# Shared expert blocks of a mixture-of-experts layer: VectorE's table chain cut into four steps inside one block, and two row buffers for TensorE

## The reference

```python
def _L0_ffn_ref(x, Ws1, bs1, Ws2, bs2, We1, be1, We2, be2, Wr, br):
    ys = _geglu(xf @ Ws1 + bs1) @ Ws2 + bs2          # shared expert: all 4096 tokens, hidden 512
    logits = (xf @ Wr + br) / TAU
    top_val, top_idx = jax.lax.top_k(logits, 2)      # two of 12 experts a token
    ...
    h = jnp.einsum('nd,edh->enh', xf, We1) + be1[:, None, :]     # experts: hidden 768
    act = _geglu(h)
    yE = jnp.einsum('enh,ehd->end', act, We2) + be2[:, None, :]
    yr = jnp.einsum('end,ne->nd', yE, w)
    return (ys + yr).reshape(B, T, Dm)
x = x + _L0_xattn_ref(_layernorm(x, axis=-1), ctx_1024, ctx_1024, mask_BxSxS2_bk1, ...)
x = x + _L0_ffn_ref(_layernorm(x, axis=-1), ...)
```

## Time and profile before

| | us |
|---|---|
| median of three runs | 1064.05 |
| the profiled execution, time | 1065.91 |
| its span in the trace | 1064.3 |
| TensorE busy | 948.2 (89%) |
| attention part ends, shared blocks begin on TensorE | 465.9 |
| first matmul of an expert | 587.1 |

### The profile page before, as it was taken

How to read it: one execution, slowest core, us unless ns; L and a number is a source line. 1 busy time by engine, 2 the same in 40 slices (tenths; PEclk the granted TensorE clock), 3 DMA queues, 4 the chain that set the end, 5 groups by cost and what they waited for, 6 DMA issues and landing times.

```text
span 1064.3 us, 26714 instructions
## 1 busy us (share of the span) xinstructions
PE 948.2 (89%) x7515; PEld 696.4 (65%) x7515; DVE 715.9 (67%) x1842; ACT 569.6 (54%) x1276; POOL 372.4 (35%) x537
## 2 busy tenths in 40 slices
PE   5578899999998888978899789999899999999996
PEld 4223444444453346767788678888688888888885
DVE  4776778888787654647686566776546577667753
ACT  3125555655555573323444556766546566667653
POOL 5210212254544362157000334444223444434342
PEclk9779999999999998989899989999999999999998
DMA  4552424273562131247644552545225445535232
GB/s 149 137 101 71 104 69 111 64 188 94 121 161 63 63 140 60 71 157 240 218 150 132 162 131 45 138 131 141 41 33 130 114 78 141 130 48 145 43 52 41
DMA packets 107926, 117.30 MB, mean 110 GB/s; under 512 B 20397, under 2 KB 99961, under 8 KB 107649
## 3 DMA queue, kind: packets, MB, share of 16 engines
q1 hardware_dynamic: 87168, 67.97, 24.0%
q0 software_dynamic: 20064, 47.20, 17.8%
q10 hardware_dynamic: 560, 0.53, 0.1%
HBM read 73.91 MB, written 38.87 MB: 106 GB/s over the span
## 4 chain that ended last, share of the span: by engine, by line
PE 39%; issue 5%; DMA 5%; DVE 4%; ACT 1%; DVEq 1%; SPq 1%; ACTq 1%; POOL 0%; POOLq 0%
PE ff_psH L2273 23%; PE ff_psY L2288 13%; DMA ff_xrow<-expert_in 2%; PE ff_psX L2223 2%; DVE ff_actf L2499 1%; PE ff_psH L2238 1%; DMA ff_xrow<-xn 1%; DVE ff_actl L2492 1%; DMA expert_in<-ff_zeros 1%; PE ff_psY L2253 1%; DMA out_dram<-ff_x 1%; DVE xl L2482 0%; ACT ff_gel L2353 0%; ACT xh L2339 0%; SPq L1966 0%
## 5 line engine op out<-in xcount | busy, mean ns | idle before, releaser
L2273 PE MATMUL ff_psH<-xh,ff_wx 128*128 128x256 f16 (+1 forms) x1776 | 272.0, 264 | 24.8 <-DVE ff_actf L2499 7.6
L2273 PE MATMUL ff_psH<-xl,ff_wx 128*128 128x256 f16 (+1 forms) x888 | 226.0, 264 | 0.0
L1126 DVE TENSOR_REDUCE fast_negm<-fast_psS 128x2 f32<-128x512 f32 x256 | 168.3, 686 | 70.9 <-PE fast_psS L514 69.6
L886 ACT ACTIVATE fast_PT<-fast_psT 128x512 f32<-128x512 f32 x256 | 147.2, 596 | 104.7 <-PE fast_psT L546 104.5
L2273 PEld LDWEIGHTS ff_psH<-xh,ff_wx 128*128 128x128 f16 x1776 | 168.5, 99 | 46.8 <-issue 21.6
L2208 POOL DMA_INDIRECT out_dram<-ff_ysc,ff_trow x78 | 124.8, 1600 | 204.0 <-ACT ff_ysc L2395 187.6
L2499 DVE SCALAR_TENSOR_TENSOR ff_actf<-ff_psH,ff_b1T,ff_gel 128x256 f32<-128x256 f32 (+1 forms) x234 | 105.6, 454 | 105.4 <-ACT ff_gel L2353 103.1
L2353 ACT ACTIVATE ff_gel<-ff_psH,ff_b1T 128x256 f32<-128x256 f32 (+1 forms) x234 | 104.8, 450 | 88.0 <-PE ff_psH L2273 73.3
L2288 PE MATMUL ff_psY<-ff_wx,ff_acth 128*128 128x256 f16 x792 | 132.0, 273 | 0.1
L2348 ACT ACTIVATE ff_acth<-ff_actf 128x256 f16<-128x256 f32 (+1 forms) x282 | 110.5, 392 | 37.2 <-DVE ff_actf L2499 35.4
L514 PE MATMUL fast_psS<-fast_Kz,fast_Qs 128*128 128x512 f16 x256 | 101.3, 401 | 32.3 <-DVE fast_negm L1126 23.7
(11 more groups left out here) (276 smaller groups left out, 1676.1 us busy)
## 6 DMA issues: line engine op xcount, KB each, us to landing
ff_st<-in_L_ffn_We_dram POOLq DMA_DIRECT2D x12, 1536.0 KB, 8.2
ff_xrow<-expert_in SPq DMA_DIRECT2D x41, 256.0 KB, 2.8
ff_st<-in_L_ffn_We_dram POOLq DMA_DIRECT2D x12, 768.0 KB, 9.7
fast_Qs<-qstk SPq DMA_DIRECT2D x48, 128.0 KB
fast_xbuf<-in_x_dram SPq DMA_DIRECT2D x8, 512.0 KB, 5.0
fast_words<-in_mask_BxSxS_bk_dram SPq DMA_DIRECT2D x8, 512.0 KB, 3.8
fast_xres<-in_x_dram SPq DMA_DIRECT2D x8, 512.0 KB, 4.1
out_dram<-fast_x1s SPq DMA_DIRECT2D x8, 512.0 KB, 5.1
```

Of the source, the lines that this page charges most:

```text
L886: nc.scalar.activation(PT[:, n % NPT, :], psT[n % 2][:], ACT.Exp).then_inc(sem["exp_done"], 1)
L1126: nc.vector.tensor_reduce(negm[:, two(b), t, 2 * p:2 * p + 2], src, AX.X, ALU.max, negate=True).then_inc(sem["max_done"], 1)
L2273: mm = nc.tensor.matmul(psH[j % stage.banks][:, (half + 1) * NB - rows:(half + 1) * NB], a[:, dt, lo:lo + P], x[:, dt, NB - rows:], start= ...
```

## The change

It does three things. (1) `tables()` is cut into `chosen_rows` (now first), `units_of`, `blocks_of` and `tables`, and these four are the `beside` steps of block 2 on VectorE: one behind each pair. `over` moves up by two places. (2) The copied rows go to two buffers by turns, `xrow[:, u]` with u = 1 for odd blocks, each with a semaphore of its own (`even_loaded`, `odd_loaded`); `load_shared(m)` waits for the transposes of block m-2 instead of m-1, and stands one block earlier in SP's stream. The experts' blocks use buffer 0, behind a wait for the transposes of block 10. (3) TensorE's blocks 0, 1 and 2 are written out, and its loop over blocks 3 to 10 runs over four pairs of blocks; SP's loops are by pairs or written out too. No work is added or left out on any engine.

```diff
-    xrow = {stage: sb(f"xrow{i}", [P, NBT, D], FP32) for i, stage in enumerate((shared, expert))}
+    xrow = sb("xrow", [P, 2, NBT, D], FP32)
...
-        def load_shared(m):
-            until(shared, "xT_mm", of(shared, "xT_mm", m))
-            sp.dma_start(xrow[shared][:], keep["xn2"][:, bass.ds((m + EARLY) * NBT, NBT), 0:D])\
-                .then_inc(shared.sem["x_loaded"], 16)
+        def load_shared(m, u):
+            until(shared, "xT_mm", of(shared, "xT_mm", m - 1))
+            sp.dma_start(xrow[:, u], keep["xn2"][:, bass.ds((m + EARLY) * NBT, NBT), 0:D])\
+                .then_inc(shared.sem["odd_loaded" if u else "even_loaded"], 16)
...
-        load_shared(1)
+        load_shared(1, 1)
         load_x1(0)
+        load_shared(2, 0)
...
-        with sp.Fori(0, 2) as m:
-            load_shared(m + 2)
+        for m in range(2):
+            load_shared(m + 3, (m + 1) % 2)
             store_out(m)
             load_x1(m + 1)
...
-        with sp.Fori(0, E // 2) as m:
-            load_shared(m + 4)
-            store_out(m + 2)
-            load_x1(m + 3)
-            zeros_after(2 * m)
-            zeros_after(2 * m + 1)
-        with sp.Fori(E // 2, NSH - 4) as m:
-            load_shared(m + 4)
+        with sp.Fori(0, E // 4) as two:
+            for k in range(2):
+                m = two * 2 + k
+                load_shared(m + 5, 1 - k)
+                store_out(m + 2)
+                load_x1(m + 3)
+                zeros_after(2 * m)
+                zeros_after(2 * m + 1)
+        load_shared(NSH - 1, 1)
+        for m in range(E // 2, NSH - 4):
             store_out(m + 2)
             load_x1(m + 3)
...
+        until(shared, "xT_mm", of(shared, "xT_mm", NSH - 1))
         load_rows(0)
...
-        shared_blocks(pe, shared_block, 3, AFTER_LISTS + 1)
+        with pe.Fori(0, (AFTER_LISTS - 2) // 2) as two:
+            for k in range(2):
+                shared_block(two * 2 + 3 + k, 1 - k)
...
         shared_blocks(dve, shared_block, 0, 2)
-        tables()
-        shared_blocks(dve, shared_block, 2, FIRST_PIECES)
+        steps_of_tables = [chosen_rows, units_of, blocks_of, tables]
+        ffn(shared, 2, bs1T, (shared, 3), add_shared, lambda j: steps_of_tables[j]())
+        shared_blocks(dve, shared_block, 3, FIRST_PIECES)
```

More of the change, by code:

```diff
@@ L1849, in start_ahead @@
     def start_ahead(self, eng):
-        begun = ("x_loaded", "xT_mm", "xh", "xl") if self.begun else ()
+        begun = ("xT_mm", "xh", "xl") if self.begun else ()
         for n, s in self.sem.items():
@@ L2107, in load_rows @@
             until(expert, "xT_mm", of(expert, "xT_mm", n))
-            sp.dma_start(xrow[expert][:], rows_at(n)[:, :, 0:D]).then_inc(expert.sem["x_loaded"], 16)
+            sp.dma_start(xrow[:, 0], rows_at(n)[:, :, 0:D]).then_inc(expert.sem["x_loaded"], 16)
         def load_meta(n):
@@ L2217, in _, with row_transposes @@
     def _(pe):
-        def row_transposes(stage, m):
-            stage.until(pe, "x_loaded", of(stage, "x_loaded", m, 16))
+        def row_transposes(stage, m, u=0):
+            if stage is expert:
+                stage.until(pe, "x_loaded", of(stage, "x_loaded", m, 16))
+            else:
+                loaded = "odd_loaded" if u else "even_loaded"
+                stage.until(pe, loaded, (m - (2 - u)) * 8 + 16)
             stage.until(pe, "xl", of(stage, "xl", m))
@@ L2293, in ffn, with shared_block @@
                     between()
-        def shared_block(m, more=None, between=None):
-            ffn(shared, m, s1, s2, more or (shared, m + 1), between=between)
-        shared_blocks(pe, shared_block, 0, 2)
+        def shared_block(m, u, more=None, between=None):
+            ffn(shared, m, s1, s2, more or (shared, m + 1, 1 - u), between=between)
+        for m in range(2):
+            shared_block(m, m)
         pe.wait_ge(b_loaded, 32)
@@ L2324, in _ @@
         pe.wait_ge(table_ready, 1)
-        shared_block(NSH - 1, (expert, 0), next_place)
+        shared_block(NSH - 1, 1, (expert, 0), next_place)
         def weights_ready(e, u, last):
@@ L2411, in _, with chosen_rows, units_of @@
         nc.vector.tensor_copy(last_pos[:], keep["row"][:, :, NT - LEFT * QT:NT]).then_inc(last_ready, 1)
-        def tables():
+        def chosen_rows():
+            dve.wait_ge(cleared, 1)
+            nc.vector.tensor_copy(tokf[:], keep["tok"][:, 0:SEEN])
+            nc.vector.tensor_copy(iota_row[:], iota_f[:])
+            then(nc.vector.tensor_tensor(chosen[:], keep["pick"][:, 0, 0:SEEN, :], keep["pick"][:, 1, 0:SEEN, :], ALU.add))
+            nc.vector.tensor_scalar(unchosen[:], chosen[:], float(-N), float(N), ALU.mult, ALU.add).then_inc(free_link, 1)
             then(nc.vector.tensor_tensor(counts[:], keep["next_row"][:], keep["region"][:], ALU.subtract))
             nc.vector.tensor_copy(ends_i[:], keep["next_row"][:])
+        def units_of():
             then(nc.vector.tensor_scalar(counts_i[:], counts[:], float(NB - 1), None, ALU.add))
@@ L2424, in tables, with blocks_of @@
             then(nc.vector.tensor_scalar(half_i[:], units_i[:], 1, None, ALU.bitwise_and))
+        def blocks_of():
             then(nc.vector.tensor_copy(half[:, 0:E], half_i[:]))
@@ L2435, in tables @@
                                     cum[:].unsqueeze(1).to_broadcast([P, NBLK + 2, E]), ALU.is_ge)
+        def tables():
             nc.vector.tensor_scalar(beyond[:], blocks[:], float(-NB), float(REGION), ALU.mult, ALU.add)
+            nc.vector.tensor_scalar(over[:], units[:], float(-2 * FEW), 0.0, ALU.add, ALU.max)
             then(nc.vector.tensor_tensor(first[:], cum[:], blocks[:], ALU.subtract))
             then(nc.vector.scalar_tensor_tensor(beyond[:], change[:], float(-UN), beyond[:], ALU.mult, ALU.add))
[L2439 removed]
             then(nc.vector.scalar_tensor_tensor(first[:], first[:], float(PLACE), units[:], ALU.mult, ALU.add))
```

13 lines of the change are left out of this document (4 added, 9 removed).

## The result

The changed kernel takes 1059.47 us (median of 14 runs, 1054.44 to 1062.93) against 1064.55 us for the kernel before in the same session (14 runs, 1060.37 to 1067.64). The ratio is 0.9950 with a 95% interval of 0.9933 to 0.9967: 5.1 us off 1064 at the middle, 3.5 to 7.1 at the ends. The profiled execution took 1058.57 us for a span of 1056.9.

What follows compares the result with a forecast made beforehand. Two TensorE holes in the shared blocks' chain (5.5 and 6.3 us) were to be had; a late load leaves 3.2 us off: 1065.91 to 1062.7, and, that execution lying 1.86 above the median, 1060.9; range 1056.4 to 1063.3.

Steps and rivals of the forecast that it cites:

- The tables in steps: VectorE's table steps between block 2's gates shrink TensorE's hole at block 2's output: 3.0 us gained (1.7 to 3.0).
- Two row buffers: Block 5's row copy goes out 6.6 us earlier, before the weights, so its transposes' 3.43 us wait goes.
- What is late next: Block 4's `ff_x` load, stuck behind block 3's store in the weights' backlog, goes out at 517.0 to 517.5.
- TensorE's new hole: Before block 5's output, 520.1 to about 522.9, 2.5 to 2.8 us; a clock fall costs 0.5 at most.
- rival B: The extra row copy pushes store and load further into the backlog, and the clock falls: 1 to 2.5 off; chance 0.12.
- Behind block 6 nothing changes: From block 6 to the experts and after, everything shifts as a whole, with nothing changed in kind.
- Rival A: Block 3's store lands early, so block 4's load is on time: 7.6 us off, partially 4 to 6; chance 0.17.
- Rival C: TensorE's two-block loop body must be refetched at each of three returns, 3 us each: median 1070; chance 0.05.

Runs made afterwards that it cites:

- the first pair: The changed kernel without further edits against the kernel before: 1059.47 us against 1064.55 us, ratio 0.9950.
- a second pair: The changed kernel against the kernel before, both with table-entry loads that assert their bounds on each engine: ratios to the unedited kernel before 0.9975 and 1.0016.
- the edit: Twelve loads of packed table entries assert their bounds on each engine, in every follow-up kernel; alone on the kernel before: 1066.39 us, ratio 1.0016.
- the second comparison: The changed kernel run again with bounds-asserting table-entry loads, against the kernel before without them: 1060.67 us, ratio 0.9975.
- the loops alone: The kernel before with only TensorE's loops written out and paired, plus bounds-asserting table-entry loads, against the kernel before: ratio 1.0016.
- the last chip: Kernel before, changed kernel, `x1` in two buffers with whole tables, and that on the kernel before, all with asserted loads: ratios 1.0023, 0.9995, 1.0002, 0.9996 to 1099.23 us.

## Why the prediction was right, and where it was not

The forecast was 1060.9 with 1056.4 to 1063.3; the median came to 1059.47. The mechanism was right, but the number owes something to luck: the stage gave less than forecast, and the rest of the timed difference has no cause on record. Point by point:

- **The tables in steps, 3.0 us at the start of block 3.** Measured 3.7 in the first pair, at clock 1.00 as assumed; the output ended 29.1 us into the stage where the forecast has 29.8 (495.7 less 465.93). VectorE ended the tables at 492.65, 32.2 in, forecast 33.2.
- **Two row buffers: the wait of 3.43 us goes, no transpose waits.** So it was. The runs add that, with one buffer of `x1`, this is the only part with a gain of its own (113.34 us against 117.22; the tables alone 117.01).
- **What is late next, the load of `x1` for block 4, issued when the backlog ends.** Right in mechanism and in time: forecast 51.1 to 51.6 us into the stage, measured 51.70 and 50.90; VectorE's wait was 7.06 and 6.58 where I had expected 3 to 5. Block 5's first gate was forecast 54.6 to 55.2 in and came at 55.4 (515.86).
- **The step that was mis-sized: TensorE's new hole of 2.5 to 2.8 us, and a fall of the clock at 0.5 at most.** Measured 4.09 and 3.60, with the clock at 0.50, and that fall costs 1.7 us. TensorE resumed at 57.1 as forecast (57.0), but it arrived at the hole 53.0 us into the stage and not 54.2: I had spread VectorE's tables over 1 us more than they took, and let block 3 lose part of its gain. That gain of 1.2 us didn't shorten anything, it only made the hole longer, and the clock fell in it. So block 6 started 62.5 in where I had 60.9 to 61.5, and the stage won 2.0 us in place of 3.2 (3.1 in a second pair, 117.22 less 114.10, whose two profiles are from different chips). The first pair has rival B's size (1 to 2.5 off) and its fall of the clock, but not its cause: the load went out within 0.1 us of the forecast's span.
- **Behind block 6 nothing changes.** Right in the sum: 481.6 against 481.5 us from the expert's transposes on. Just behind them the changed kernel has an idle time of 2.08 us where the kernel before has 1.81. Behind the longer one the clock did fall:

```profile
583.88 0.23 PE L2282 MATMUL ff_psH<-xh,ff_wx 128*128 128x128 f16 x1 [2.08 <-DVE ff_actf L2518]
```

```profile
585.00:587.00 2.00, 2.00 (x22) 2.00 (x19) 1.75 (x8) 1.00 (x4) 0.11 (x1) 0.50 0.01 4
```

The next transposes come 1.1 us later than in the kernel before, counted from those of the expert's first rows; by the third after them 1.0 us of it is made up.

- **Rival A, the store let through sooner.** Refuted: 10.79 and 10.32 us for it, until 511.9 in the first profile and 512.4 in the second. It was issued 1.6 us earlier than before (40.66 us into the stage against 42.25), where the forecast had it 0.5 us later and rival A up to 1 us earlier, and still it ended about when the weights did.
- **Rival C, slower by instruction loading.** Refuted. Between 505 and 568, where the loop returns three times, the changed kernel has no packet of q8, and no idle time of TensorE of 0.2 us or more ended by "issue" in blocks 3 to 10. Two packets of q8 lie ahead of that, one at the loop's start (488 to 490) and one in its first pass (500 to 503); TensorE didn't stand still for either. What hung on the Trainium skill's rule of two pages (Runtime: NRT & Kernel Launch, section Instruction fetch mechanics) did not happen; the 128 KB of the page Advanced Engine Details and Errata, section ISA Cache, agree with what ran.
- **The sums.** The starts of block 6 that the working gives, 526.8 to 527.4 against 530.46, are 3.1 to 3.7 us off, not 2.9 to 3.6, and B's smaller gain of 1 us ends at 1063.05, not 1063.3. Neither changes the outcome.
- **The time.** That the median came out 1.4 us below the forecast is not its merit. The pair of medians differs by 5.1 us (3.5 to 7.1) and the stage by 2.0 to 3.1; with the stage's gain alone the median would have been some 1061.5 to 1062.5, an estimate from 1064.55, inside the range but above the forecast. With the edit taken off, the second comparison gives 4.4, by both intervals some 2 to 7. The attention part explains the first pair of profiles, since it ended anywhere from 459.75 to 465.93 us in ten profiles, the lowest with the loops alone and the highest in the kernel before; it doesn't explain a median. Whether one to two us are won outside the shared stage stays open: the medians on the last chip, 2.6 us apart, speak against it, though weakly, since their intervals overlap, and no run shows a place for it.

## What to carry to other kernels

A gain ahead of a transfer that goes out at a fixed time is only idle time moved; before costing a faster stretch, ask which load the next block needs and what has to end before it may be issued. A store and the load behind it through one buffer turn any backlog in the DMA engines into a wait of the compute engines; a second buffer took 8 us more here, with the backlog left as it was, while moving the large transfer only moved the collision. And where TensorE must wait, a hole behind which its clock has fallen from 2.4 to 1.2 GHz costs more than its length, 1.7 us more here.

## What the runs showed of the hardware

- A store of 256 KB took 2.1 to 2.6 us by itself, and 9.2 to 10.8 us to its landing beside the 2.3 MB of weights from the other queue (10.79 in the kernel after, where the weights landed up to 11.4 us after their issue at 499.7, at 511.1); from its issue to that of the load behind it passed 8.8 to 11.3 us. Beside the two weight loads apart, 1536 and 768 KB, it took 7.3 and 6.4 us. The store had company in SP's own queue too: two writes of zeros of 264 KB each and a row copy of 256 KB went out just ahead of it, and with the weights held back it took 4.38 us. The Trainium skill (DMA: Bandwidth & Descriptors, section Queues, rings and completion order) says that a DMA engine takes the queues that have work in turn, a packet at a time; the smaller queue would then be expected to end first, and here the store ended 0.8 us after the weights (511.9 against 511.1). Why, no run shows.
- How long TensorE stood idle in one piece didn't by itself tell whether the granted clock would fall. Behind every idle time of 3.17 us or more that began at 1.00 it fell to 0.50 (3.17, 3.18, 3.21, 3.43, 3.60, 3.82, 4.09, 4.79, 7.50). Behind most of 1.30 to 2.11 us it stayed at 1.00 for the next microseconds, and once behind 2.46. But it also fell behind 1.56 us with 0.86 us idle shortly before, and behind 2.08, 2.39 and 2.76 us.
- The chip of the last four runs ran the three kernels that also ran elsewhere 3.2 to 3.5% slower, with the stall shown above. ScalarE had single waits of up to 15.3 us that the profile puts down to nothing on this core; VectorE waited up to 9.4 us without a releaser and up to 15.3 behind ScalarE, and TensorE up to 13.6 behind VectorE. Only GpSimd's scatters went on at their own pace (one in 1.28 us, as on the other chips), and the DMA engines were 0.30 busy. The cause is open.
